# The last block of a cross-attention kernel, taken in two halves of its queries

## The chip, the cores and the metric

One Trainium2 chip, one of its cores. The metric is the device time of one execution in microseconds (us). TensorE (PE) multiplies matrices, VectorE (DVE), ScalarE (ACT) and GpSimd (POOL) work on the elements of a tile, and the queues of SyncE (SP) and ScalarE issue the transfers (DMA). Each engine runs its own list of instructions in the order in which they are written, and semaphores tie the lists together: an instruction whose semaphore isn't there yet holds everything behind it on its engine.

## What is computed

Cross-attention of 4 x 1024 queries on 77 keys for each batch, 16 heads of 16 columns, all in float32:

```
q, k, v = x W_Q^T, ctx W_K^T, ctx W_V^T          x: (4, 1024, 256), ctx: (4, 77, 256), 16 heads of 16
scores  = q k^T / 4,  -1e9 where mask == 1
p       = softmax(scores)
concat  = p v                                     (4, 1024, 256)
out     = concat W_O^T + x
result  = (out - mean) * rsqrt(var + 1e-5) * gamma + beta      (mean and var over the 256 columns)
```

## The kernel before

The 4096 queries are cut into 8 **blocks** of 512 (n = 0 to 7, N = 8). A block has 16 heads, worked off in 8 **steps** of two heads (a pair), and in 4 **quads** of four heads (t = 0 to 3). Engines work on several blocks at once. For the last two blocks only this matters:

- **Scores** (PE, L912, `scores`): two matmuls a step, keys on the partitions, 512 queries as columns, into two of six PSUM banks. The last steps rotate over three pairs of banks (`pair_bank`), so step k waits for the exponentials of step k - 3 (`heads_gone`).
- **Exponentials** (ACT, L551, `exp`): one instruction for the 77 x 1024 scores of a pair, to `probs`.
- **Values** (PE, L920, `values`): four matmuls, one for each head of a quad, into the four strips of 32 partitions of the one bank `pv_ps`. The sum of the exponentials comes along as an extra column of v. The next quad may write `pv_ps` only when DVE has transposed the one before out of it.
- **Turn** (DVE, L670 and L672, `turn`): `pv_ps` is transposed in squares of 32 to `ctx_q`, and the reciprocals of the sums are taken. **Norm** (POOL, L364, `norm`) multiplies the two into `ctx_n`. **Turn back** (DVE, L678, `turn_back`) transposes two quads (one of two column halves) to `ctx_e`.
- **Output** (PE, L930, `project_out`): 4 fp32 matmuls for each half of the rows, into the bank `work_ps`. **Residual** (DVE, L684) adds x from `y`. **Stats** (DVE, L690 and L695) take mean and variance.
- **Moments** (POOL, L373 to L378): four small instructions make 1/sqrt(var + eps) and the shift. **Apply** (ACT, L557) scales and shifts the four tiles of a block. **Times gamma** (POOL, L385) and **plus beta** (POOL, L391), two instructions each for a block. SP then stores the block (`store_y`, L282).

The last block (n = 7) ends in another way. Its fourth quad is taken in two halves of 256 queries, in two PSUM banks (`last_values`, L1048), and DVE does the whole way of each half itself: transpose, reciprocal, product, transpose back (`turn_last`, L707 to L715). The output matmuls (L1053) go into four PSUM tiles `last_ps`, x is added by a matmul with the identity (L1057), and DVE does statistics, gamma and beta on PSUM (L811 to L827). POOL gives only 1/sqrt(var + eps) for each half (L485). The block is stored in two halves from ACT's queue (L614).

The order of the work around the end is written out by hand, for each engine. POOL, from the last norm of block 6 on: moments(5), norm(7, 0), plus beta(4), times gamma(5) first half, norm(7, 1), times gamma(5) second half, norm(7, 2), moments(6), times gamma(6) in both halves, the two L485, plus beta(6) in both halves. Plus beta(5) is on DVE (L700), ahead of the last quad. SP stores blocks 5 and 6 when their plus beta is done.

Of the kernel before, what the change touches and what calls it, by code (L numbers as in the profile page):

```python
# [8 lines left out]
ALU = mybir.AluOpType  # L9
# [3 lines left out]
P = 128  # L13
BATCH = 4
SEQ = 1024
D = 256
# [44 lines left out]
Y_RING = 4  # L61
R_RING = 3
# [52 lines left out]
def cross_attention(nc, x, x_cols, ctx_cols, mask_cols, w_q, w_k, w_v, w_o, gamma, beta, out):  # L115
    stack = ExitStack()
    with stack:
# [6 lines left out]
        def sem(name):  # L124
            return stack.enter_context(nc.semaphore(name))
# [61 lines left out]
        last_ps = [banks[:, 0, 0:D], banks[:, 1, 0:D], work_ps[:, 0:D], banks[:, 2, 0:D]]  # L187

        last_pv = [pv_ps[:, 0:BLOCK // 2], banks[:, 3, 0:BLOCK // 2]]
# [25 lines left out]
        ident_ready, last_scaled, last_shifted = sem("ident_ready"), sem("last_scaled"), sem("last_shifted")  # L215
        last_bn, last_mv, last_ve, last_rstd = sem("last_bn"), sem("last_mv"), sem("last_ve"), sem("last_rstd")
# [120 lines left out]
        def _(pool):  # L337
# [132 lines left out]
            norm(N - 2, 3)  # L470
            moments(N - 3)
            norm(N - 1, 0)
            plus_beta(N - 4, 1)
            times_gamma(N - 3, 0)
            norm(N - 1, 1)
            times_gamma(N - 3, 1)
            norm(N - 1, 2)

            moments(N - 2)
            for half in range(2):  # L480
                times_gamma(N - 2, half)
            for half in range(2):
                two = slice(2 * half, 2 * half + 2)
                pool.wait_ge(last_ve, half + 1)
                nc.gpsimd.tensor_tensor(rstd_last[:, two], var_eps_last[:, two], minus_half[:, two], ALU.pow).then_inc(last_rstd, 1)  # L485
            for half in range(2):
                plus_beta(N - 2, half)
# [4 lines left out]
        def _(act):  # L492
# [92 lines left out]
            for n in range(N):  # L585
                for s in range(STEPS):
# [19 lines left out]
                    at = {N - 2: 5, N - 1: 3}.get(n, 6)  # L606
                    if s in (at, at + 1) and n >= 2:
                        for t in (2 * (s - at), 2 * (s - at) + 1):
                            apply(n - 2, t)
            for t in range(TILES):  # L610
                apply(N - 2, t)
# [8 lines left out]
        def _(dve):  # L620
# [76 lines left out]
            def plus_beta(m, half):  # L697
                rows = y[m % Y_RING][:, 2 * half:2 * half + 2, :]
                dve.wait_ge(y_gamma, 2 * m + half + 1)
                nc.vector.tensor_tensor(rows, rows, beta_sb[:, :].unsqueeze(1).to_broadcast([P, 2, D]), ALU.add).then_inc(y_beta, 1)  # L700

            def turn_last(half):
                chunks = slice(half * CHUNKS // 2, (half + 1) * CHUNKS // 2)
                m, t = N - 1, QUADS - 1
                dve.wait_ge(pv_done, QUADS * m + t + half + 1)
                dve.wait_ge(ctx_normed, QUADS * m + t)
                nc.vector.transpose(ctx_q[:, t % 2, chunks, :], last_pv[half]).then_inc(pv_turned, 1)  # L707
                dve.wait_ge(pv_turned, QUADS * m + t + half + 1)
                nc.vector.reciprocal(rden[:, t % 2, chunks], ctx_q[:, t % 2, chunks, DK]).then_inc(rden_ready, 1)
                dve.wait_ge(rden_ready, QUADS * m + t + half + 1)  # L710
                nc.vector.tensor_tensor(ctx_n[:, 1, chunks, DK:2 * DK], ctx_q[:, t % 2, chunks, 0:DK],
                                        rden[:, t % 2, chunks].unsqueeze(2).to_broadcast([P, CHUNKS // 2, DK]),
                                        ALU.mult).then_inc(ctx_normed, 1)
                dve.wait_ge(ctx_normed, QUADS * m + t + half + 1)
                nc.vector.transpose(ctx_e[m % 2][:, 1, half * BLOCK // 2:(half + 1) * BLOCK // 2], ctx_n[:, 1, chunks, :]  # L715
                                    ).then_inc(ctx_e_ready, 1)
# [77 lines left out]
            turn(n, 0)  # L794
            residual(n - 1, 0)
            turn(n, 1)
            stats(n - 1, 0)
            turn_back(n, 0)
            residual(n - 1, 1)
            turn(n, 2)  # L800
            stats(n - 1, 1)
            for half in range(2):
                plus_beta(n - 2, half)
            for half in range(2):
                turn_last(half)
            m, rows = n, y[n % Y_RING]
            for half in range(2):
                two = slice(2 * half, 2 * half + 2)
                for t in (2 * half, 2 * half + 1):
                    dve.wait_ge(out_done, 2 * m + t + 1)  # L810
                    nc.vector.bn_stats(bn_last[:, t, :], last_ps[t]).then_inc(last_bn, 1)  # L811
                    dve.wait_ge(last_bn, t + 1)
                    nc.vector.bn_aggr(mean_var_last[:, t, :], bn_last[:, t, :]).then_inc(last_mv, 1)
                dve.wait_ge(last_mv, 2 * half + 2)
                nc.vector.tensor_scalar(var_eps_last[:, two], mean_var_last[:, two, 1], EPS, None, ALU.add).then_inc(last_ve, 1)
                if half == 0:
                    for t in range(2):
                        nc.vector.scalar_tensor_tensor(out=last_ps[t], in0=last_ps[t], scalar=mean_var_last[:, t, 0:1],
                                                       in1=gamma_sb[:, :], op0=ALU.subtract, op1=ALU.mult).then_inc(last_scaled, 1)
            for t in (2, 3):  # L820
                nc.vector.scalar_tensor_tensor(out=last_ps[t], in0=last_ps[t], scalar=mean_var_last[:, t, 0:1],
                                               in1=gamma_sb[:, :], op0=ALU.subtract, op1=ALU.mult).then_inc(last_scaled, 1)
            for half in range(2):
                dve.wait_ge(last_rstd, half + 1)
                for t in (2 * half, 2 * half + 1):
                    dve.wait_ge(last_scaled, t + 1)
                    done = nc.vector.scalar_tensor_tensor(out=rows[:, t, :], in0=last_ps[t], scalar=rstd_last[:, t:t + 1],  # L827
                                                          in1=beta_sb[:, :], op0=ALU.mult, op1=ALU.add)
                done.then_inc(last_shifted, 1)
# [4 lines left out]
        def _(pe):  # L834
# [210 lines left out]
            def last_values(half):  # L1045
                cols = slice(half * BLOCK // 2, (half + 1) * BLOCK // 2)
                for j in range(4):
                    last = nc.tensor.matmul(last_pv[half][32 * j:32 * (j + 1), :], v_all[:, n // PER_BATCH, 4 * (QUADS - 1) + j, :],  # L1048
                                            probs[:, 2 * (QUADS - 1) + j // 2, j % 2, cols], start=True, stop=True)
                last.then_inc(pv_done, 1)  # L1050

            def last_out(v, t):
                return nc.tensor.matmul(last_ps[t], ctx_e[n % 2][:, v, t * P:(t + 1) * P], wo_t[:, v, :],  # L1053
                                        start=(v == 0), stop=(v == HALVES - 1))

            def last_residual(t):
                nc.tensor.matmul(last_ps[t], ident32[:, :], rows[:, t, :], start=False, stop=False)  # L1057

            scores(n, 0)
            scores(n, 1)  # L1060
            values(n - 1, 3)
            scores(n, 2)
            values(n, 0)
            scores(n, 3)
            pe.wait_ge(out_ready, 2 * (n - 1))
            project_out(n - 1, 0)
            scores(n, 4)
            values(n, 1)
            scores(n, 5)
            pe.wait_ge(out_ready, 2 * (n - 1) + 1)  # L1070
            project_out(n - 1, 1)
            scores(n, 6)
            values(n, 2)
            scores(n, 7)
            pe.wait_ge(s_x[n % Y_RING], 16 * (n // Y_RING + 1))
            pe.wait_ge(ident_ready, 1)
            pe.wait_ge(exp_done, HEADS * n + 12)
            pe.wait_ge(ctx_e_ready, HALVES * n + 1)
            last_out(0, 0)
            last_out(0, 1)  # L1080
            pe.wait_ge(exp_done, HEADS * N)
            pe.wait_ge(pv_turned, QUADS * n + QUADS - 1)
            last_values(0)
            last_values(1)
            last_residual(0)
            last_residual(1)
            for t in range(TILES):
                if t == 2:
                    pe.wait_ge(out_ready, 2 * n)
                if t >= 2:  # L1090
                    last_out(0, t)
                    last_residual(t)
                if t % 2 == 0:
                    pe.wait_ge(ctx_e_ready, HALVES * n + 2 + t // 2)
                last_out(1, t).then_inc(out_done, 1)
# [39 lines left out]
```

## Time and profile before

| | |
|---|---|
| median of 3 runs | 186.15 us (182.85, 186.15, 188.56) |
| the profiled execution, its own time | 182.77 us |
| its span, first to last instruction | 181.0 us |
| granted TensorE clock, mean over the span | 0.976 of 2.4 GHz |
| PE busy | 159.6 us (88%), 1224 matmuls |
| DVE busy | 136.9 us (76%), 305 instructions |
| ACT busy | 103.2 us (57%), 188 instructions |
| POOL busy | 102.5 us (57%), 125 instructions |

The shares are means over the whole span, and most of the span is the same loop over blocks. The change touches the last 30 us. There the timelines of the engines and the chain of waits are read: a timeline line gives the start, the duration of the merged piece, the operation with its tiles, the number of instructions, and in brackets how long the engine had sat idle before it and what released it. Busy times of neighbours on one engine overlap a little, since an instruction starts before the one in front of it has ended; the distance between two starts is what an instruction costs in a row of others.

### The profile page before, as it was taken

The page shows a single profiled execution, that of the slowest core. Times are in us where ns is not written, and L with a number is a line of the kernel's source. Part 1 is how long each engine was busy: PE and PEld are TensorE (multiplying, and loading weights), DVE is VectorE, ACT ScalarE, POOL GpSimd, SP SyncE. Part 2 cuts the span into 40 slices and gives each one's busy share as a digit, 9 for nine tenths or more (in the row PEclk, how much of TensorE's full clock was granted, in tenths as well). Part 3 has the DMA queues.
Part 4 walks back from the last instruction along what each step waited for, and adds up shares of the span by engine and source line. Part 5 has one row for each costly group of instructions (what it writes and reads, how often), then busy time and mean ns, then how long its engine had stood idle before and what let it go on. Part 6 is the DMA issues. An engine that isn't in the chain of part 4 may idle for free.

```text
span 181.0 us, 3572 instructions
## 1 busy us (share of the span) xinstructions
PE 159.6 (88%) x1224; PEld 87.9 (49%) x1224; DVE 136.9 (76%) x305; ACT 103.2 (57%) x188; POOL 102.5 (57%) x125
## 2 busy tenths in 40 slices
PE   7698877889579999999999999999999897999830
PEld 7455534444244565456545654565366462264520
DVE  0779755885958579788978897889989966748990
ACT  3224154673366565658765876587777659586400
POOL 7000761242835451448597959754954787865692
PEclk9999999999999999999999999999999999699995
DMA  4949947779867987973686665647551033020205
GB/s 158 384 120 184 257 86 224 182 167 230 188 170 217 281 237 216 253 201 85 196 274 181 193 198 145 187 164 205 141 182 53 4 121 116 0 116 4 116 0 232
DMA packets 21829, 30.17 MB, mean 167 GB/s; under 512 B 3436, under 2 KB 17356, under 8 KB 21812
## 3 DMA queue, kind: packets, MB, share of 16 engines
q1 hardware_dynamic: 20692, 28.19, 55.8%
q10 hardware_dynamic: 1120, 1.76, 2.9%
q8 instruction: 10, 0.16, 0.4%
q14 instruction: 7, 0.06, 0.1%
HBM read 11.28 MB, written 4.19 MB: 85 GB/s over the span
## 4 chain that ended last, share of the span: by engine, by line
PE 52%; DVE 12%; POOL 9%; issue 9%; DMA 8%; ACT 6%; ACTq 1%; POOLq 0%; SPq 0%; DVEq 0%
PE pv_ps L920 12%; PE work_ps L857 11%; PE work_ps L930 9%; PE scores_ps L912 9%; PE scores_ps L878 6%; DMA R<-neg_max_t 4%; DMA x_t<-in_x_cols 4%; POOL y L385 3%; DVE ctx_q L670 2%; PE scores_ps L857 2%; DVE neg_max L662 2%; DVE q L651 2%; POOL rstd L376 2%; POOL ctx_n L364 2%; DVE bn L690 1%
## 5 line engine op out<-in xcount | busy, mean ns | idle before, releaser
L547 ACT ACTIVATE probs<-scores_ps 77x512 f32<-77x512 f32 x108 | 57.7, 589 | 36.7 <-PE scores_ps L912 31.4
L662 DVE TENSOR_REDUCE neg_max<-scores_ps 128x6 f16<-128x462 f32 (+1 forms) x84 | 45.2, 565 | 11.0 <-PE scores_ps L878 11.0
L912 PE MATMUL scores_ps<-R,kb 126*77 126x512 f16 x128 | 39.5, 388 | 4.1 <-DMA R<-neg_max_t 3.0
L357 POOL TENSOR_TENSOR q<-q 128x512 f16<-128x512 f32 x14 | 16.2, 1161 | 43.4 <-ACT q L505 43.4
L878 PEld LDWEIGHTS scores_ps<-kb,R 125*128 125x128 f16 x512 | 26.7, 98 | 28.5 <-DVE neg_max L662 10.8
L920 PE MATMUL pv_ps<-probs,v_all 77*32 77x512 f32 x248 | 33.8, 618 | 2.2 <-ACT probs L551 1.0
L364 POOL TENSOR_TENSOR ctx_n<-ctx_q,rden 128x256 f32<-128x256 f32 x31 | 19.5, 628 | 23.6 <-DVE rden L672 23.5
L878 PE MATMUL scores_ps<-kb,R 125*128 125x77 f16 x512 | 31.2, 199 | 1.3 <-DVE neg_max L662 1.1
L670 DVE STREAM_TRANSPOSE ctx_q<-pv_ps 128x512 f32<-128x512 f32 x31 | 22.1, 712 | 9.3 <-PE pv_ps L920 8.9
L930 PE MATMUL work_ps<-wo_t,ctx_e 128*128 128x256 f32 x112 | 27.4, 388 | 0.0
L857 PE MATMUL work_ps<-x_t,wq_t 128*128 128x512 f32 x48 | 23.6, 614 | 0.4
L930 PEld LDWEIGHTS work_ps<-wo_t,ctx_e 128*128 128x128 f32 x112 | 21.3, 194 | 3.5 <-issue 0.2
L385 POOL TENSOR_TENSOR y<-y,gamma_sb 128x512 f32<-128x512 f32 x14 | 17.8, 1274 | 2.8 <-ACT y L557 2.8
L912 PEld LDWEIGHTS scores_ps<-R,kb 126*77 126x77 f16 x128 | 11.2, 117 | 15.8 <-issue 5.8
L557 ACT ACTIVATE y<-y,shift,rstd 128x256 f32<-128x256 f32 x28 | 15.1, 591 | 2.9 <-POOL shift L378 2.9
L391 POOL TENSOR_TENSOR y<-y,beta_sb 128x512 f32<-128x512 f32 x12 | 15.2, 1269 | 0.0
L505 ACT ACTIVATE q<-q 128x512 f16<-128x512 f32 x16 | 10.0, 626 | 7.5 <-DVE q L651 5.5
L551 ACT ACTIVATE probs<-scores_ps 77x1024 f32<-77x1024 f32 x10 | 9.9, 1016 | 4.1 <-PE scores_ps L912 4.1
L684 DVE TENSOR_TENSOR y<-work_ps,y 128x512 f32<-128x512 f32 x14 | 9.5, 680 | 3.6 <-PE work_ps L930 3.6
L342 POOL TENSOR_SCALAR eq<-mask_i 77x512 f16<-77x512 int32 x6 | 11.6, 1929 | 1.0 <-DMA mask_i<-in_mask_cols 1.0
L857 PEld LDWEIGHTS work_ps<-x_t,wq_t 128*128 128x128 f32 x48 | 8.2, 190 | 6.6 <-issue 5.7
L678 DVE STREAM_TRANSPOSE ctx_e<-ctx_n 128x512 f32<-128x512 f32 x15 | 10.5, 703 | 1.0 <-POOL ctx_n L364 1.0
(88 smaller groups left out, 158.7 us busy)
## 6 DMA issues: line engine op xcount, KB each, us to landing
R<-mask_t SPq DMA_DIRECT2D x12, 616.0 KB
R<-q SPq DMA_DIRECT2D x48, 128.0 KB
x_t<-in_x_cols SPq DMA_DIRECT2D x8, 512.0 KB, 6.2
y<-in_x SPq DMA_DIRECT2D x8, 512.0 KB, 4.6
out<-y SPq DMA_DIRECT2D x7, 512.0 KB, 2.6
mask_i<-in_mask_cols SPq DMA_DIRECT2D x8, 154.0 KB
out<-y ACTq DMA_DIRECT2D x2, 256.0 KB, 2.0
kb<-k SPq DMA_DIRECT2D x12, 38.5 KB, 2.9
```

The lines of the kernel that those rows point to most:

```text
L357: nc.gpsimd.tensor_tensor(q16[:, e, 1, :], q32[:, e, :], q16[:, e, 0, :], ALU.subtract).then_inc(q_low, 1)
L364: nc.gpsimd.tensor_tensor(ctx_n[:, v, :, u * DK:(u + 1) * DK], ctx_q[:, t % 2, :, 0:DK], rden[:, t % 2, :].unsqueeze(2).to_broadcast([P, C ...
L385: nc.gpsimd.tensor_tensor(rows, rows, gamma_sb[:, :].unsqueeze(1).to_broadcast([P, 2, D]), ALU.mult).then_inc(y_gamma, 1)
L391: nc.gpsimd.tensor_tensor(rows, rows, beta_sb[:, :].unsqueeze(1).to_broadcast([P, 2, D]), ALU.add).then_inc(y_beta, 1)
L547: nc.scalar.activation(probs[:, s, head % 2, :], banks[0:KEYS, head % SCORES_RING, :], ACT.Exp).then_inc(exp_done, 1)
L662: nc.vector.tensor_reduce(to[:, t, lo:hi], max_ps[u % MAX_RING][:, 0:(hi - lo) * KEYS].rearrange("p (h k) -> p h k", k=KEYS), AX.X, ALU.ma ...
L670: nc.vector.transpose(ctx_q[:, t % 2, :, :], pv_ps[:, :]).then_inc(pv_turned, 1)
L857: last = nc.tensor.matmul(bank, wq_t[:, t, e * P:(e + 1) * P], x_t[m % X_RING][:, t, :], start=(t == 0), stop=(t == HALVES - 1))
L878: last = nc.tensor.matmul(max_ps[u % MAX_RING][:, (h - lo) * KEYS:(h - lo + 1) * KEYS], R[m % R_RING][0:MAX_ROW, h, t * P:(t + 1) * P], kb ...
L912: nc.tensor.matmul(banks[0:KEYS, bank, :], kb[:, 2 * s + i, n // PER_BATCH, :], R[n % R_RING][:, 2 * s + i, :], start=True, stop=True).the ...
L920: last = nc.tensor.matmul(pv_ps[32 * j:32 * (j + 1), :], v_all[:, n // PER_BATCH, 4 * t + j, :], probs[:, 2 * t + j // 2, j % 2, :], start ...
L930: last = nc.tensor.matmul(work_ps[:, i * D:(i + 1) * D], ctx_e[n % 2][:, v, q0:q0 + P], wo_t[:, v, :], start=(v == 0), stop=(v == HALVES - 1))
```

## The change

Block 7 goes through its four quads twice: parts g = 0 to 3 are the quads for the first 256 queries, g = 4 to 7 the same quads for the other 256.

- PE: each `part_scores` has four matmuls of 256 columns (a part's four heads fill the same two banks that a pair filled before), each `part_values` four of 256 columns, into the first half of `pv_ps`. A part's values wait for the transposition of the part before. Once parts 0 to 3 are turned back (`part_e` 1 and 2), x and the output matmuls of the first half go to `work_ps`; those of the second half to a pair of score banks.
- ACT: eight exponentials of 77 x 1024, as before, each writing half of the queries of four heads. The applies of block 5 follow parts 3 and 4.
- DVE: eight half-size turns and four half-size turn-backs; the product of the last part alone is DVE's. `last_moments(0)` stands ahead of turn 7, `last_shift(0)` behind the last turn-back.
- POOL: seven half-size norms, plus beta(5) moved here from DVE, and another order: the two times gamma of block 6 come after the first L485, and the second L485 between the two plus beta of block 6.

The core of the diff:

```
 (POOL)
-            norm(N - 1, 0)
+            norm_part(0)
             plus_beta(N - 4, 1)
-            norm(N - 1, 1) ... norm(N - 1, 2)
-            moments(N - 2)
-            for half in range(2):
-                times_gamma(N - 2, half)
-            for half in range(2):
-                ... rstd_last ...
-            for half in range(2):
-                plus_beta(N - 2, half)
+            norm_part(1)
+            times_gamma(N - 3, 0)
+            norm_part(2)
+            norm_part(3)
+            times_gamma(N - 3, 1)
+            norm_part(4)
+            moments(N - 2)
+            norm_part(5)
+            plus_beta(N - 3, 0)
+            norm_part(6)
+            plus_beta(N - 3, 1)
+            rstd_of_last(0)
+            for half in range(2):
+                times_gamma(N - 2, half)
+            plus_beta(N - 2, 0)
+            rstd_of_last(1)
+            plus_beta(N - 2, 1)

 (DVE)
-            turn(n, 0); residual(n - 1, 0); turn(n, 1); stats(n - 1, 0); turn_back(n, 0)
-            residual(n - 1, 1); turn(n, 2); stats(n - 1, 1); plus_beta(n - 2, 0 and 1)
-            turn_last(0); turn_last(1); ... statistics and outputs of the last block
+            turn_part(0)
             residual(n - 1, 0)
+            turn_part(1)
+            turn_back_part(0, 0)
+            turn_part(2)
+            residual(n - 1, 1)
+            turn_part(3)
             stats(n - 1, 0)
+            turn_back_part(0, 1)
+            turn_part(4)
             stats(n - 1, 1)
+            turn_part(5)
+            turn_back_part(1, 0)
+            turn_part(6)
+            last_moments(0)
+            turn_part(7)
+            norm_last_part()
+            turn_back_part(1, 1)
+            last_shift(0)
+            last_moments(1)
+            last_shift(1)

 (PE)
+            part_scores(0); part_scores(1); values(n - 1, 3); part_scores(2); part_values(0); part_scores(3)
+            project_out(n - 1, 0); part_values(1); part_scores(4); project_out(n - 1, 1)
+            part_values(2); part_scores(5); part_values(3); part_scores(6); part_values(4); part_scores(7)
+            last_x(0, work_ps)                      # x of both tiles of the first half
+            last_out(0, 0); last_out(0, 1)
+            part_values(5)
+            last_out(1, 0); last_out(1, 1)          # after part_e 2
+            part_values(6)
+            last_x(2, ...); last_x(3, ...)
+            last_out(0, 2); last_out(0, 3)          # after part_e 3
+            part_values(7)
+            last_out(1, 2); last_out(1, 3)          # after part_e 4
```

## Rows read from the trace of the kernel before

**Rows 1.** Chain that ended last, order of time: start us, us, what; final links.
```profile
171.12 2.50 POOL y L385 x2
173.62 0.66 POOL rstd_last L485
...
175.32 2.45 POOL y L391 x2
```

**Rows 2.** Timeline of the queues: block 6's store, block 7's two; page, to landing.
```profile
177.80 0.33 SPq L282 DMA_DIRECT2D out<-y  x1
...
176.14 1.13 ACTq L614 DMA_DIRECT2D out<-y  x2
...
out<-y ACTq DMA_DIRECT2D x2, 256.0 KB, 2.0
```

**Rows 3.** Timeline of POOL, 156 to 175 us.
```profile
156.27 0.23 POOL L373 TENSOR_SCALAR var_eps<-mean_var 128x4 f32<-128x4 f32 x1 [0.21 <-DVE mean_var L695]
...
158.21 0.62 POOL L364 TENSOR_TENSOR ctx_n<-ctx_q,rden 128x256 f32<-128x256 f32 x1
...
167.34 0.58 POOL L373 TENSOR_SCALAR var_eps<-mean_var 128x4 f32<-128x4 f32 x1 [0.21 <-DVE mean_var L695]
...
168.60 1.04 POOL L376 TENSOR_TENSOR rstd<-var_eps,minus_half 128x4 f32<-128x4 f32 x1
169.71 0.20 POOL L378 TENSOR_TENSOR shift<-rstd,neg_mean 128x4 f32<-128x4 f32 x1
...
174.63 0.70 POOL L485 TENSOR_TENSOR rstd_last<-var_eps_last,minus_half 128x2 f32<-128x2 f32 x1 [0.35 <-DVE var_eps_last L815]
```

**Rows 4.** Timeline of PE, 153 to 170 us.
```profile
153.22 1.06 PE L920 MATMUL pv_ps<-probs,v_all 77*32 77x512 f32 x8 [1.04 <-ACT probs L551]
...
155.22 1.86 PE L920 MATMUL pv_ps<-probs,v_all 77*32 77x512 f32 x8 [0.38 <-DVE ctx_q L670]
...
157.88 2.34 PE L930 MATMUL work_ps<-wo_t,ctx_e 128*128 128x256 f32 x8
...
162.03 1.89 PE L930 MATMUL work_ps<-wo_t,ctx_e 128*128 128x256 f32 x8
163.76 0.60 PE L912 MATMUL scores_ps<-R,kb 126*77 126x512 f16 x2
...
167.10 0.64 PE L1048 MATMUL pv_ps<-probs,v_all 77*32 77x256 f32 x8 [0.33 <-ACT probs L551]
167.56 0.61 PE L1048 MATMUL scores_ps<-probs,v_all 77*32 77x256 f32 x8
```

**Rows 5.** Windows: stretch, length, busy of each engine, granted clock, DMA share, GB/s.
```profile
154.00:160.00 6.00, 5.62 (x24) 2.64 (x21) 3.39 (x9) 3.78 (x6) 5.12 (x8) 0.72 0.00 0
```

**Rows 6.** Timeline of DVE, 162 to 170 us.
```profile
162.63 0.69 DVE L690 BATCH_NORM_STATS2 bn<-y 128x6 f32<-128x256 f32 x2
...
163.46 0.71 DVE L678 STREAM_TRANSPOSE ctx_e<-ctx_n 128x512 f32<-128x512 f32 x1
164.09 0.65 DVE L684 TENSOR_TENSOR y<-work_ps,y 128x512 f32<-128x512 f32 x1
...
167.17 1.26 DVE L700 TENSOR_TENSOR y<-y,beta_sb 128x512 f32<-128x512 f32 x2
168.35 0.44 DVE L707 STREAM_TRANSPOSE ctx_q<-pv_ps 128x256 f32<-128x256 f32 x1
168.82 0.20 DVE L709 RECIPROCAL rden<-ctx_q 128x8 f32<-128x8 f32 x1
169.06 0.29 DVE L711 TENSOR_TENSOR ctx_n<-ctx_q,rden 128x128 f32<-128x128 f32 x1
169.38 0.45 DVE L715 STREAM_TRANSPOSE ctx_e<-ctx_n 128x256 f32<-128x256 f32 x1
```

**Rows 7.** Timeline of DVE, 27 to 47 us: two runs of L719, the same size.
```profile
27.77 0.47 DVE L719 TENSOR_SCALAR kb<-ident 77x1232 f16<-77x1232 f16 x1
...
46.55 0.86 DVE L719 TENSOR_SCALAR kb<-ident 77x1232 f16<-77x1232 f16 x1
```

More of the change, by code:

```diff
@@ L583, in _ @@
             turn_first_max(1)
-            for n in range(N):
+            for n in range(N - 1):
                 for s in range(STEPS):
@@ new lines, in turn_part @@
+            def turn_part(g):
+                half, t = g // QUADS, g % QUADS
+                chunks = slice(half * HALF_CHUNKS, (half + 1) * HALF_CHUNKS)
+                dve.wait_ge(part_pv, g + 1)
+                if g < 2:
+                    dve.wait_ge(ctx_normed, QUADS * (N - 2) + t + 3)
+                elif t >= 2:
+                    dve.wait_ge(part_normed, g - 1)
+                nc.vector.transpose(ctx_q[:, t % 2, chunks, :], pv_ps[:, 0:HALF]).then_inc(part_turned, 1)
+                dve.wait_ge(part_turned, g + 1)
+                nc.vector.reciprocal(rden[:, t % 2, chunks], ctx_q[:, t % 2, chunks, DK]).then_inc(part_rden, 1)
@@ new lines, in last_moments @@
+            def last_moments(half):
+                two = slice(2 * half, 2 * half + 2)
+                for t in (2 * half, 2 * half + 1):
+                    dve.wait_ge(last_out_done, 2 if half == 0 else t + 1)
+                    nc.vector.bn_stats(bn_last[:, t, :], last_ps[t]).then_inc(last_bn, 1)
+                for t in (2 * half, 2 * half + 1):
+                    dve.wait_ge(last_bn, t + 1)
+                    nc.vector.bn_aggr(mean_var_last[:, t, :], bn_last[:, t, :]).then_inc(last_mv, 1)
+                dve.wait_ge(last_mv, 2 * half + 2)
+                nc.vector.tensor_scalar(var_eps_last[:, two], mean_var_last[:, two, 1], EPS, None, ALU.add).then_inc(last_ve, 1)
+                for t in (2 * half, 2 * half + 1):
+                    nc.vector.scalar_tensor_tensor(out=last_ps[t], in0=last_ps[t], scalar=mean_var_last[:, t, 0:1],
+                                                   in1=gamma_sb[:, :], op0=ALU.subtract, op1=ALU.mult).then_inc(last_scaled, 1)
@@ new lines, in last_shift @@
+            def last_shift(half):
+                dve.wait_ge(last_rstd, half + 1)
+                for t in (2 * half, 2 * half + 1):
+                    dve.wait_ge(last_scaled, t + 1)
+                    done = nc.vector.scalar_tensor_tensor(out=y[(N - 1) % Y_RING][:, t, :], in0=last_ps[t],
+                                                          scalar=rstd_last[:, t:t + 1], in1=beta_sb[:, :],
+                                                          op0=ALU.mult, op1=ALU.add)
+                done.then_inc(last_shifted, 1)
@@ L804, in _ @@
[L804 to L829, printed above, removed]
+            turn_part(5)
@@ L1056, in last_residual, with part_scores @@
[L1056 to L1060, printed above, removed]
+            def part_scores(g):
+                half, t = g // QUADS, g % QUADS
+                if g == 0:
+                    pe.wait_ge(s_nm, 16 * n)
+                if g < 3:
+                    pe.wait_ge(exp_done, heads_gone(PAIRS * n + g))
+                else:
+                    pe.wait_ge(part_exp, g - 2)
+                for j in range(4):
+                    done = nc.tensor.matmul(part_ps[g][0:KEYS, j // 2, (j % 2) * HALF:(j % 2 + 1) * HALF],
+                                            kb[:, 4 * t + j, n // PER_BATCH, :],
+                                            R[n % R_RING][:, 4 * t + j, half * HALF:(half + 1) * HALF], start=True, stop=True)
+                done.then_inc(part_scored, 1)
@@ new lines, in part_values @@
+            def part_values(g):
+                half, t = g // QUADS, g % QUADS
+                if g == 0:
+                    pe.wait_ge(pv_turned, QUADS * n)
+                else:
+                    pe.wait_ge(part_turned, g)
+                pe.wait_ge(part_exp, g + 1)
+                for j in range(4):
+                    done = nc.tensor.matmul(pv_ps[32 * j:32 * (j + 1), 0:HALF], v_all[:, n // PER_BATCH, 4 * t + j, :],
+                                            probs[:, 2 * t + j // 2, j % 2, half * HALF:(half + 1) * HALF], start=True, stop=True)
+                done.then_inc(part_pv, 1)
@@ L1061, in _, with last_x, last_out @@
+            def last_x(lo, to):
+                tiles = rows[:, lo:lo + to.shape[-1] // D, :]
+                nc.tensor.matmul(to, ident32[:, :], tiles, start=True, stop=False)
+            def last_out(v, t, stop=False):
+                return nc.tensor.matmul(last_ps[t], ctx_e[n % 2][:, v, t * P:(t + 1) * P], wo_t[:, v, :], start=False, stop=stop)
+            part_scores(0)
+            part_scores(1)
             values(n - 1, 3)
-            scores(n, 2)
-            values(n, 0)
-            scores(n, 3)
+            part_scores(2)
@@ L1098 @@
+            pe.wait_ge(part_e, 2)
+            last_out(1, 0)
+            last_out(1, 1, stop=True).then_inc(last_out_done, 2)
+            part_values(6)
+            last_x(2, last_ps[2])
+            last_x(3, last_ps[3])
+            pe.wait_ge(part_e, 3)
+            last_out(0, 2)
+            last_out(0, 3)
+            part_values(7)
+            pe.wait_ge(part_e, 4)
+            for t in (2, 3):
+                last_out(1, t, stop=True).then_inc(last_out_done, 1)
 def kernel(**inputs):
```

128 lines of the change are left out of this document (63 added, 65 removed).

## The prediction

> **What bounds the kernel now.** I read the tail alone, since nothing ahead of block 7's first values changes. The chain of waits shows the end: applies of block 6 on ACT, then on POOL times gamma, an inverse root, plus beta [rows 1]. Plus beta ends at 177.77 us, SP issues the store at 177.80 [rows 2], and the span ends at 181.0: 3.23 us from the last POOL instruction to the end. Block 7's own second store is issued by 177.27 [rows 2] and lands 2.0 us later [rows 2]: 179.3, 1.7 us of slack. So **the end belongs to block 6 and to POOL**, not to block 7, which the change is about. The timelines of POOL, PE and DVE give the durations; the windows give the clock, whose mean from 154 to 160 us is 0.72 [rows 5]. With the levels 1.2 and 2.4 GHz that is 3.4 us at the lower one; values that take 1.86 us instead of 1.06 at 155.22 and a projection of 2.34 instead of 1.89 at 157.88 [rows 4] put it at about 155.3 to 158.7, after PE had idled 1.04 and 0.38 us [rows 4]. PE's work up to 155.2 stays the same, so I keep this stretch where it is.
>
> **PE up to the second projection.** Before, the first half of block 6's projection starts at 157.88 and the second at 162.03 [rows 4]: 4.15 us for it, two score steps and one quad of values. In front of it now stands a half-size part. At full clock a quad is 1.06 us and a half 0.64, with 0.46 between the starts of two halves [rows 4]; at half clock that is 0.9 instead of 1.8. So the projection starts 1.0 us earlier, at 156.9 (its input, block 6's second turn-back, is there at 156.8 as before), but loses 0.5 of that by running longer at half clock. Between the two projections one quad has become a part (-0.5) and one score step has gone behind (-0.5). The second projection then starts at 157.9 - 1.0 + 0.5 + 4.15 - 1.0 = 160.5 and ends 1.73 later (start distance, [rows 4]), at 162.2: **1.5 us earlier than before**. Eight exponentials of the same size and the same columns of scores are no change; ACT waits on PE here and hides its own work.
>
> **DVE to the statistics of block 6.** Behind the projection come values 2 (0.64, ends 162.9) and on DVE, back to back: turn 2, residual, turn 3, stats half 0, turn-back, turn 4, stats half 1. A half turn costs 0.47 to its reciprocal and about 0.13 for that, 0.6 [rows 6]; residual 0.6, stats 0.83, half turn-back 0.37 to 0.45 (all [rows 6]); the last stats take 1.0 to their end. Sum: 3 x 0.6 + 0.6 + 0.83 + 0.37 + 1.0 = 4.6, so the statistics end at 167.5. Before, moments of block 6 start at 167.34 [rows 3]; now at **167.6, +0.25**. The lead of 1.5 us is eaten by two more half turns and a turn-back ahead of the statistics.
>
> **POOL from there to the end** is the sum that decides. Against before:
>
> - moments of block 6: 2.57 us before (167.34 to 169.91), but 1.94 for the same four instructions of block 5 (156.27 to 158.21) [rows 3]. The slow ones lay beside DVE's plus beta (167.17 to 168.43, [rows 6]), which is gone: -0.6.
> - norm parts 5 and 6 now stand behind moments. A norm of 256 elements takes 0.62 [rows 3], one of 512 elements (gamma, beta) 1.25 [rows 1], so time goes with elements: 0.31 to 0.35 each, bounds 0.31 and 0.62. I take 0.35, as POOL's 4-element instruction still takes 0.20: +0.7.
> - plus beta of block 5, moved here from DVE, where it took 1.26: two of 1.24 [rows 1]: **+2.5**.
> - gamma waited for the applies, which wait for moments: moments end 169.91, gamma starts 171.12 [rows 3, 1]. Now the norms and plus beta fill that gap: -1.2.
> - the second root waited 0.35 for DVE [rows 3]; now it stands behind the first plus beta of block 6: -0.35.
>
> From 167.6: 1.95 + 0.35 + 1.23 + 0.35 + 1.23 + 0.66 (root) + 2.46 (gamma) + 1.23 + 0.66 + 1.25 = 11.4, so POOL ends at 179.0, against 177.77: 0.25 - 0.6 + 0.7 + 2.5 - 1.2 - 0.35 = +1.3, +1.2 by start times. Stores as before, 3.23 us. But the two stores (block 7's second half at 178.7, block 6 at 179.0) now lie 0.3 apart, where it was 0.9; between nothing and 0.3 for that, I take 0.1: **+1.3 us**. Store of block 5 is issued at 172.8, clear of both.
>
> **Block 7's own path**, to see that it stays inside. First half: part 5's norm waits on POOL until moments are done (169.5), the turn-back behind it starts at 169.9, turn 6 behind that at 170.3. Statistics and scaling of the first half follow (its outputs stood ready from 168.8), then turn 7 at 172.8, DVE's product and turn-back (0.20 + 0.29 + 0.45 and latencies, [rows 6]) to 174.3. PE, idle for 2.5 us, does the last outputs (two of a projection's four tile products, half of its 1.73 us, and 0.16 to the end) by 175.4. Variance of the second half at 176.3, but POOL takes its root only at 177.05, behind plus beta: 0.8 us of slack. The shifts end at 178.7, the store is issued by 179.05 and lands at 181.05, 1.1 us ahead of the other.
>
> **The sum**: profiled execution 182.77 + 1.3 = 184.1 us. That execution is near the fastest of the three runs (182.85); their median is 186.15, 3.4 us higher for reasons that no trace shows, so I carry the difference over: **187.4 us**, +0.7%. A measurement of this kernel tells about 2% (3.7 us) from no change.
>
> **Rivals.**
>
> 1. *The last round trip becomes the bound.* DVE's product (ctx_q times rden, two SBUF inputs) at 173.5 falls in POOL's times gamma (173.4 to 174.6). For a block between the two: one L719 took 0.86 us instead of 0.47 [rows 7], and POOL's small L373 0.58 instead of 0.23 while DVE ran plus beta [rows 3, 6]. Against: L711 ran in its 0.29 us inside POOL's 1.04 us root [rows 3, 6]. If it waits out the gamma, +1.1 us; and if PE's clock falls in the then 3.6 us of idleness, these two products cost 0.86 more. It decides once both exceed the 0.8 us of slack: +1.2 on the forecast, 188.6 us. The Trainium skill ("SBUF — State Buffer", section "SBUF: two separate sides") says that such a DVE instruction and a GpSimd one that reads SBUF exclude each other for a whole instruction; by it the wait occurs and the sum is the 188.6 of this rival if the clock falls too, 187.8 if not. The trace agrees in L719 and L373, and speaks against in L711.
> 2. *Slower by over 2%: half pieces cost what whole ones do.* Eight trips PE to DVE to PE go over one bank. At whole-size prices the four parts of values ahead of the statistics cost 0.5 more each, the four turns 0.3, norm parts 5 and 6 0.27: 2.0 + 1.2 + 0.5 = 3.7, less some 0.3 where PE waits anyway: 3.4 over my forecast, 190.8. With whole-size turns and norms it passes 2% once the values of a part start 0.7 us apart. Against: halves took 0.61 to 0.64 [rows 4] and 0.44 [rows 6] where wholes take 1.06 and 0.71.
> 3. *The waits on POOL close up.* POOL's work from the first norm part (158.2, [rows 3]) is 7 x 0.35 + 9 x 1.24 + 1.95 + 2 x 0.68 = 16.9 us; my schedule has 3.8 us of waits in 20.8. Without any, the end is 158.2 + 16.9 + 3.2 = 178.3, 2.6 us under before: 183.5 us. For it: the statistics could come earlier if the lower clock does not fall there. Against: the norm parts wait on PE, in order. Even this floor is only 1.4%: **a gain over 2% has no place** in this tail.
>
> **Chances.** Forecast within half a microsecond or so 0.50; rival 1 0.21; rival 3, in part or whole, 0.15; rival 2 0.12; something else 0.02. Range 183.5 (rival 3) to 190.0: rival 1 at 188.6 with norms at their upper bound (+0.5) and values parts 0.6 apart (+0.4) on top, 189.5, and 0.5 for a stretch of lower clock; rival 2 is left out. Faster by over 2%: 0.08, only from the scatter of the runs. Slower by over 2%: rival 2 and the rest of the scatter, 0.14. Within 2%: 0.78.
>
> **What would show it.** In the new profile: POOL without a gap over 0.2 us from its moments of block 6 (167 to 168) to its last plus beta (near 179), and the chain ending in that plus beta and SP's store; the moments in 1.95 us; norm parts near 0.35; the second projection starting near 160.5; L719-like stretching of DVE's last product, or not; PE idle for 2 to 3 us before its last two tiles. I am wrong if block 7's store ends the span, if POOL still waits before its gamma, or if the statistics of block 6 end before 166.5 or after 168.5.

## The result and the profile after

The changed kernel took 189.45 us (median of 4 executions, 188.75 to 189.72), the kernel before 185.09 us (median of 4, 182.85 to 188.56): ratio 1.0281, 95% interval 1.0233 to 1.0330. **Slower by 2.8%**, where +0.7% was forecast. Medians, here and below, take every execution; the ratios and their intervals leave out those more than 1.5% above the fastest of their kernel. The profiled execution took 189.72 us with a span of 187.6 us, against 182.77 and 181.0.

To compare the tails, both are counted from one event that the change leaves alone: the start of PE's values for the last quad of block 6, at 153.22 us before [rows 4]. In the changed kernel (timeline of PE):

```profile
157.42 1.07 PE L976 MATMUL pv_ps<-probs,v_all 77*32 77x512 f32 x8 [1.03 <-ACT probs L578]
...
164.07 1.89 PE L986 MATMUL work_ps<-wo_t,ctx_e 128*128 128x256 f32 x8
...
175.30 0.64 PE L1123 MATMUL pv_ps<-probs,v_all 77*32 77x256 f32 x8
179.08 2.04 PE L1132 MATMUL scores_ps<-wo_t,ctx_e 128*128 128x256 f32 x4 [3.15 <-DVE ctx_e L763]
```

That start is 4.2 us late. Two score steps of the changed block 7 have run by then (155.35), but these values wait for an exponential of block 6, and the delay is much older: the same values of an early block start at 56.36 us before and at 60.55 in the changed kernel, where nothing has been changed yet. The **tail**, from there to the end of the span, is 30.2 us, where it was 27.8. So 6.6 us between two profiles fall into 4.2 ahead of the change and 2.4 behind it. The 4.2 are the clock; windows of the changed kernel (stretch, length, busy time of PE, PEld, DVE, ACT and POOL, granted clock, DMA share, GB/s):

```profile
40.00:50.00 10.00, 7.17 (x52) 3.18 (x52) 7.11 (x14) 3.61 (x7) 5.54 (x5) 0.97 0.79 215
50.00:60.00 10.00, 9.21 (x42) 3.89 (x43) 3.40 (x6) 3.36 (x6) 2.88 (x3) 0.52 0.74 210
```

The clock fell from its level of 2.4 GHz to that of 1.2 GHz at about 49.5 us, while PE waited 3.35 us for the row of maxima of block 1, and came back at about 59.6; in the profile of before it stayed up there, after a wait of 3.00 us, and fell at 155 us [rows 5].

In the tail, POOL's timeline is the one to hold against [rows 3] and [rows 1]:

```profile
171.17 0.23 POOL L381 TENSOR_SCALAR var_eps<-mean_var 128x4 f32<-128x4 f32 x1 [0.45 <-DVE mean_var L732]
...
173.06 0.40 POOL L485 TENSOR_TENSOR ctx_n<-ctx_q,rden 128x128 f32<-128x128 f32 x1
173.42 1.28 POOL L399 TENSOR_TENSOR y<-y,beta_sb 128x512 f32<-128x512 f32 x1
...
175.01 1.28 POOL L399 TENSOR_TENSOR y<-y,beta_sb 128x512 f32<-128x512 f32 x1
176.39 0.71 POOL L492 TENSOR_TENSOR rstd_last<-var_eps_last,minus_half 128x2 f32<-128x2 f32 x1
177.07 2.53 POOL L393 TENSOR_TENSOR y<-y,gamma_sb 128x512 f32<-128x512 f32 x2
179.56 1.26 POOL L399 TENSOR_TENSOR y<-y,beta_sb 128x512 f32<-128x512 f32 x1
182.09 0.71 POOL L492 TENSOR_TENSOR rstd_last<-var_eps_last,minus_half 128x2 f32<-128x2 f32 x1 [1.27 <-DVE var_eps_last L775]
182.77 1.26 POOL L399 TENSOR_TENSOR y<-y,beta_sb 128x512 f32<-128x512 f32 x1
```

POOL works without a break of note from 171.17 to 180.82, as forecast, and then waits 1.27 us for the variance of block 7's second half, with half of block 6's plus beta queued behind the root. DVE shows why that variance is late:

```profile
175.39 0.92 DVE L775 TENSOR_SCALAR var_eps_last<-mean_var_last 128x2 f32<-128x2 f32 x1
...
177.72 0.76 DVE L750 TENSOR_TENSOR ctx_n<-ctx_q,rden 128x128 f32<-128x128 f32 x1
178.58 0.45 DVE L763 STREAM_TRANSPOSE ctx_e<-ctx_n 128x256 f32<-128x256 f32 x1
...
181.84 0.17 DVE L775 TENSOR_SCALAR var_eps_last<-mean_var_last 128x2 f32<-128x2 f32 x1
```

The same instruction on two elements takes 0.92 us beside POOL's plus beta (175.01 to 176.29) and 0.17 when POOL does nothing; the last product takes 0.76 us beside times gamma, where it took 0.29 [rows 6]. PE idles 3.15 us and does its last two fp32 matmuls (a row counts each as two, x4) in 2.04 us; the same in the middle of the tail took 1.03 (170.22 us). Block 6's store is the last: POOL ends at 184.03, the span at 187.6.

### The profile page after: what moved, and what is told of

Same layout as the page of the kernel before. It is cut to its first block, busy times and chain, and to the rows that moved or that the text cites. A ratio compares the mean times of both kernels' runs of the same rounds, so it can differ in the third digit from the quotient of the medians.

```text
span 187.6 us, 3661 instructions
## 1 busy us (share of the span) xinstructions
PE 164.4 (88%) x1262; PEld 90.4 (48%) x1262; DVE 137.5 (73%) x309; ACT 103.4 (55%) x188; POOL 105.0 (56%) x131
## 4 chain that ended last, share of the span: by engine, by line
PE 51%; DVE 13%; POOL 11%; DMA 9%; issue 9%; ACT 3%; SPq 1%; POOLq 0%; ACTq 0%; DVEq 0%
PE work_ps L913 12%; PE pv_ps L976 10%; PE work_ps L986 9%; PE scores_ps L968 8%; PE scores_ps L934 6%; DMA R<-neg_max_t 4%; DMA x_t<-in_x_cols 3%; POOL y L393 3%; POOL ctx_n L372 2%; DMA R<-q 2%; PE scores_ps L913 2%; POOL y L399 2%; DVE neg_max L699 2%; DVE ctx_q L707 2%; POOL rstd L384 2%
## 5 line engine op out<-in xcount | busy, mean ns | idle before, releaser
L934 PEld LDWEIGHTS scores_ps<-kb,R 125*128 125x128 f16 x512 | 27.5, 100 | 30.0 <-DVE neg_max L699 10.8
L968 PE MATMUL scores_ps<-R,kb 126*77 126x512 f16 x112 | 35.4, 393 | 4.5 <-DMA R<-neg_max_t 3.4
L934 PE MATMUL scores_ps<-kb,R 125*128 125x77 f16 x512 | 31.9, 201 | 1.4 <-DVE neg_max L699 1.1
L976 PE MATMUL pv_ps<-probs,v_all 77*32 77x512 f32 x224 | 30.7, 621 | 1.8 <-ACT probs L578 1.0
L372 POOL TENSOR_TENSOR ctx_n<-ctx_q,rden 128x256 f32<-128x256 f32 x28 | 17.6, 627 | 21.4 <-DVE rden L709 21.4
L707 DVE STREAM_TRANSPOSE ctx_q<-pv_ps 128x512 f32<-128x512 f32 x28 | 19.9, 710 | 8.4 <-PE pv_ps L976 8.0
L913 PE MATMUL work_ps<-x_t,wq_t 128*128 128x512 f32 x48 | 25.3, 653 | 0.4
L399 POOL TENSOR_TENSOR y<-y,beta_sb 128x512 f32<-128x512 f32 x14 | 17.8, 1271 | 0.0
L968 PEld LDWEIGHTS scores_ps<-R,kb 126*77 126x77 f16 x112 | 9.8, 119 | 11.3 <-ACT probs L574 3.9
L727 DVE BATCH_NORM_STATS2 bn<-y 128x6 f32<-128x256 f32 x28 | 10.0, 398 | 0.0
```

The source lines that it names most:

```text
L372: nc.gpsimd.tensor_tensor(ctx_n[:, v, :, u * DK:(u + 1) * DK], ctx_q[:, t % 2, :, 0:DK], rden[:, t % 2, :].unsqueeze(2).to_broadcast([P, C ...
L707: nc.vector.transpose(ctx_q[:, t % 2, :, :], pv_ps[:, :]).then_inc(pv_turned, 1)
L913: last = nc.tensor.matmul(bank, wq_t[:, t, e * P:(e + 1) * P], x_t[m % X_RING][:, t, :], start=(t == 0), stop=(t == HALVES - 1))
L934: last = nc.tensor.matmul(max_ps[u % MAX_RING][:, (h - lo) * KEYS:(h - lo + 1) * KEYS], R[m % R_RING][0:MAX_ROW, h, t * P:(t + 1) * P], kb ...
L968: nc.tensor.matmul(banks[0:KEYS, bank, :], kb[:, 2 * s + i, n // PER_BATCH, :], R[n % R_RING][:, 2 * s + i, :], start=True, stop=True).the ...
L976: last = nc.tensor.matmul(pv_ps[32 * j:32 * (j + 1), :], v_all[:, n // PER_BATCH, 4 * t + j, :], probs[:, 2 * t + j // 2, j % 2, :], start ...
```

## Experiments

Times are medians; the column beside them has the median of the kernel before, run in the same set, and kernels of different sets are best compared by their distance from it. The tail is taken from each profile.

| kernel | median us | before, same set | block 6's last values start | span | tail |
|---|---|---|---|---|---|
| before, first profile | 185.09 | (itself) | 153.22 | 181.0 | 27.8 |
| before, again | 184.47 | 184.52 | 156.34 | 182.8 | 26.5 |
| b_warm | 182.11 | 184.36 | 154.38 | 180.8 | 26.4 |
| b_warm2 | 183.29 | 184.52 | 155.40 | 181.8 | 26.4 |
| b_poolbeta | 182.67 | 184.83 | 152.74 | 179.7 | 27.0 |
| changed, first profile | 189.45 | 185.09 | 157.42 | 187.6 | 30.2 |
| changed, again | 188.56 | 184.83 | 156.67 | 186.9 | 30.2 |
| a_warm | 185.64 | 184.36 | 153.20 | 183.0 | 29.8 |
| a_beta | 185.26 | 184.36 | 154.15 | 183.9 | 29.75 |
| a_root | 184.62 | 184.36 | 153.00 | 181.9 | 28.9 |
| a_pve | 185.58 | 184.83 | 154.10 | 183.5 | 29.4 |
| a_tailwarm | 186.01 | 184.83 | 156.61 | 185.9 | 29.3 |
| a_best | 184.85 | 184.52 | 153.92 | 183.2 | 29.3 |
| a_full | 184.35 | 185.13 | 153.58 | 182.4 | 28.8 |

**The early wait, b_warm and a_warm.** The same edit in both kernels:

```
 scores(n, s), elif s == 0:
+    if n == 1:
+        pe.wait_ge(exp_done, HEADS + 1 - SCORES_RING)
+        for _ in range(40):
+            nc.tensor.matmul(banks[:, HEADS % SCORES_RING, 0:P], zeros16[:, :], zeros16[:, :], start=True, stop=True)
     pe.wait_ge(s_nm, 16 * n)
```

> The kernel before, with 40 small matmuls of zeros put on PE in its first long wait (47.5 to 50.7 us, for the row of negative maxima of block 1), into a score bank that is free; nothing that is computed changes. Theory A (PE's clock falls in this wait in some executions, whatever the last block does, and that made 4.2 of the 6.6 us between the two profiles): the clock stays up at 47 to 60 us, the time is that of the fastest executions, 182.5 to 183.5 us, with little scatter. Theory B (the wait has nothing to do with the difference, the change itself slows the whole program): no change in the median, 185 us, scatter as before.

> The changed kernel with the same 40 small matmuls in the same wait. Theory A: block 6's last values start near 153.2 us again (157.4 in the changed kernel without them) and the time falls by 4.2 us, to about 185.4 us; what is left over the kernel before with the same matmuls is the tail alone, 2.4 us by the two profiles (1.3 us was forecast for it). Theory B: still 189 us.

182.11 us (ratio to before 0.9877, 0.9804 to 0.995) and 185.64 us (1.0083, 1.004 to 1.0127). The changed kernel's values start at 153.20 again: the 4.2 us are the clock's (mean 1.00 from 50 to 60 us, where it was 0.52), theory A holds. Between the two: 3.5 us of medians, 3.4 of tail, more than the 2.4 of the first pair of profiles. b_warm has the lowest median of all, 2.25 us under the kernel before of its set.

**Both kernels again.**

> The changed kernel as it is, once more beside the kernel before, for the granted clock of every execution. Theory A1 (the early fall of the clock at 49 us is a matter of the single execution): part of the executions near 185.3 us with a mean clock of 0.97 or more, as with the matmuls of zeros in the early wait, the others near 189.5 with 0.955; the median of many comes down to 186 to 188. Theory A2 (the changed program meets the fall in every execution): all near 189.4 us with 0.955.

> The kernel before, unchanged, as a kernel of its own: a second profile of it. Theory A1 (the early wait for the row of negative maxima is as long in both kernels and the clock falls by chance): a wait of 2.6 to 3.8 us, as in all profiles taken so far. Theory A3 (the early wait is longer in the changed kernel: 3.35 and 3.48 us, against 3.00, and just past what the clock stands): again 2.9 to 3.1 us, with the clock up, and mean clocks of 0.973 to 0.985 in most executions.

The changed kernel: 188.56 us, single executions 185.67, 187.29, 188.10, 189.01, 189.61 and 191.98, so it is probably not bound to the fall; but the lowest had a mean clock of 0.968, not the 0.97 of A1, the median lies above A1's 186 to 188, and only the first, at 189.01, has a profile (ratio 1.0135, 1.0061 to 1.0208). The kernel before: 184.47 us, and A3 as it was put, with the clock up, is refuted. Timeline of PE, kernel before, second profile:

```profile
50.84 1.07 PE L912 MATMUL scores_ps<-R,kb 126*77 126x512 f16 x2 [3.12 <-DMA R<-neg_max_t]
...
52.23 1.94 PE L920 MATMUL pv_ps<-probs,v_all 77*32 77x512 f32 x8
...
156.34 1.06 PE L920 MATMUL pv_ps<-probs,v_all 77*32 77x512 f32 x8 [1.04 <-ACT probs L551]
```

Here **the kernel before meets the early fall too**, after 3.12 us of waiting (still less than the 3.35 and 3.48 of the changed kernel), and its values start at 156.3. The later fall is missing, and the tail is 26.5 us, as in b_warm and b_warm2. So the first profile of before, on which the forecast stood, had its fall in the tail (27.8 us); this one, at 184.58 us, lies at the median.

**One part alone in the old kernel, b_poolbeta.**

```
 (DVE)  -            for half in range(2): plus_beta(n - 2, half)
 (POOL)              moments(N - 2)
        +            plus_beta(N - 3, 0); plus_beta(N - 3, 1)
```

> b_warm (the kernel before with matmuls of zeros in the early wait) with one part of the change alone: plus beta of block 5 moved from DVE to POOL, behind moments of block 6. The forecast's terms: +2.5 for the two additions, -1.2 for the wait for the applies that they fill, -0.6 for the moments that no longer lie beside DVE's additions: +0.7 us over b_warm, up to 1.3 if the moments stay slow. If POOL's work were not the bound of the old tail: 0.

182.67 us, +0.56 on b_warm, but only 0.1 by the distances from the kernel before of each set (-2.16, -2.25); the tail decides, 26.96 against 26.42, +0.54. Timelines of POOL and DVE:

```profile
165.56 0.23 POOL L373 TENSOR_SCALAR var_eps<-mean_var 128x4 f32<-128x4 f32 x1 [0.21 <-DVE mean_var L697]
...
167.44 2.55 POOL L391 TENSOR_TENSOR y<-y,beta_sb 128x512 f32<-128x512 f32 x2
169.95 2.48 POOL L385 TENSOR_TENSOR y<-y,gamma_sb 128x512 f32<-128x512 f32 x2
...
170.44 0.80 DVE L815 TENSOR_SCALAR var_eps_last<-mean_var_last 128x2 f32<-128x2 f32 x1
```

Moments fast, the wait filled, 2.5 us added: three terms of the forecast's sum stand. The run also shows the collisions in the old last block, where only this part of the change is in: DVE's L815 took 0.17 us before (172.31) and takes 0.80 beside times gamma. Of DVE's two last products, 0.29 us each before, the second (168.12) takes 0.74 beside plus beta, the first (166.75) still 0.29 beside POOL's small root.

**The other way, a_beta**: plus beta of block 5 back on DVE in a_warm.

> The one before this, with plus beta of block 5 back on DVE (one half ahead of turn 5, one behind it) and off POOL. Theory C (the tail is late because of a chain that goes through DVE's variance and last product, which wait for POOL's long instructions, and through PE's restart at the lower clock): only 0.5 to 1.0 us better than a_warm, since the last product is freed by some 0.9 us and nothing else. Theory D (POOL's amount of work is the bound, as forecast): 2.0 to 2.5 us better.

Tail 29.75 us, nothing gained on 29.8; the median 0.4 lower. POOL spends what it was relieved of in waits:

```profile
171.67 0.40 POOL L485 TENSOR_TENSOR ctx_n<-ctx_q,rden 128x128 f32<-128x128 f32 x1 [1.13 <-DVE rden L747]
172.72 0.70 POOL L492 TENSOR_TENSOR rstd_last<-var_eps_last,minus_half 128x2 f32<-128x2 f32 x1 [0.65 <-DVE var_eps_last L778]
...
178.45 0.71 POOL L492 TENSOR_TENSOR rstd_last<-var_eps_last,minus_half 128x2 f32<-128x2 f32 x1 [1.30 <-DVE var_eps_last L778]
```

POOL's amount of work alone, the bound of my forecast, is refuted as the bound of the changed tail. Theory C's half microsecond came and was lost again: PE's last matmuls start 0.4 us earlier than in a_warm (21.25 against 21.66 after block 6's last values), but take 2.07 us, where the clock in a_warm fell only half way through them (1.64).

**The root behind both plus beta, a_root.**

```
             plus_beta(N - 2, 0)
-            rstd_of_last(1)
             plus_beta(N - 2, 1)
+            rstd_of_last(1)
```

> a_warm with POOL's root for the second half of block 7 put behind both plus beta of block 6, not between them. Theory C: the root came late anyway (POOL waited 1.27 us for the variance), so it loses nothing, block 6's store leaves 1.9 us earlier and block 7's second store ends the span: 1.3 to 1.6 us better than a_warm. Theory D (POOL's work back to back is the bound, the root's place is worth only its own 0.7 us for block 6 and costs block 7 0.5 us): 0.3 us better or less.

184.62 us, 1.0 under a_warm, tail 28.9, 0.9 under it: less than the 1.3 of theory C, three times theory D. Block 6 no longer waits for block 7's variance. Timelines of PE, DVE and POOL:

```profile
174.66 1.13 PE L1136 MATMUL scores_ps<-wo_t,ctx_e 128*128 128x256 f32 x4 [3.14 <-DVE ctx_e L763]
...
176.51 1.14 DVE L775 TENSOR_SCALAR var_eps_last<-mean_var_last 128x2 f32<-128x2 f32 x1
...
177.73 0.71 POOL L492 TENSOR_TENSOR rstd_last<-var_eps_last,minus_half 128x2 f32<-128x2 f32 x1
```

What theory C left out is that block 7's root now stands behind all of plus beta, which ends at 177.62 us; the shift behind it, and the store that ends the span, follow. L775 collides again (1.14 us) but ends at 177.65, with that plus beta, so by itself it cost less than 0.1 us.

**PE kept busy in its last wait, a_tailwarm**: 45 matmuls of zeros behind `part_values(7)` in a_warm.

> a_warm with 45 more small matmuls of zeros on PE in its last long wait (before the last two output products), into a score bank that is free. Theory C (the restart at the lower clock is one link of the chain that sets the end): the last four fp32 matmuls take 1.0 to 1.1 us, not 1.6 to 2.0, POOL's wait for the variance (0.86 to 1.3 us) nearly vanishes, 0.6 to 0.9 us better than a_warm. Theory D (POOL's amount of work is the bound): no difference.

```profile
175.06 2.69 PE L1175 MATMUL scores_ps<-zeros 128*128 128x128 f16 x45
178.28 1.13 PE L1136 MATMUL scores_ps<-wo_t,ctx_e 128*128 128x256 f32 x4 [0.53 <-DVE ctx_e L763]
```

1.13 us instead of 2.04, POOL's wait 0.35; tail 29.3, 0.9 under the changed kernel, but 0.5 under a_warm, in whose restart the clock fell half way (1.64 us). The medians hardly show it (186.01, which is 1.18 over the kernel before, where a_warm is 1.28 over): single executions lie between 183.97 and 188.00.

**var + eps on POOL, a_pve** (in a_warm).

```
 rstd_of_last: +  nc.gpsimd.tensor_scalar(var_eps_last[:, two], mean_var_last[:, two, 1], EPS, None, ALU.add)
 last_moments: -  nc.vector.tensor_scalar(var_eps_last[:, two], mean_var_last[:, two, 1], EPS, None, ALU.add)
```

> a_warm with var + eps of block 7 taken from DVE (L775) and given to POOL, in front of its root. Theory E (DVE's small instruction and its last product each waited for a long POOL instruction on SBUF to end): DVE has no 0.9 us instruction any more, turn 7 starts 0.75 us earlier, the last product falls before POOL's times gamma and takes 0.3 us, not 0.76, PE waits some 2 us, not 3.1, and its clock stays up; 0.5 to 1.0 us better than a_warm though POOL has 0.6 us more to do. Rival F (the two are slow for a reason of their own, no collision): the last product still takes 0.76 us, and the time is 0 to 0.6 us worse.

```profile
173.57 0.29 DVE L752 TENSOR_TENSOR ctx_n<-ctx_q,rden 128x128 f32<-128x128 f32 x1
...
174.47 2.07 PE L1137 MATMUL scores_ps<-wo_t,ctx_e 128*128 128x256 f32 x4 [1.85 <-DVE ctx_e L765]
```

The product, now beside POOL's root and no longer beside gamma (which starts at 174.04), takes 0.29 us; PE waits 1.85 us. That is theory E, but the clock fell all the same, and the tail gains 0.4; the median is 0.75 over the kernel before, where a_warm is 1.28 over.

**All of it, a_best and a_full.** a_best: matmuls of zeros in three waits, var + eps on POOL, root last. a_full: plus beta on DVE as well. b_warm2: b_warm with 18 matmuls of zeros ahead of block 6's last values.

> b_warm with 18 more small matmuls of zeros on PE in the wait of 1.0 us ahead of block 6's last values, after which the clock fell in the profile of the kernel before (154 to 160 us, mean 0.72). If that fall costs 1.4 us where it happens: the median falls to 181.5 us or less and the executions lie closer together, about 2.8 us under the kernel before. If the fall at 155 us is rare in b_warm anyway: 182.1 us as b_warm.

> The changed kernel with all that helped it: matmuls of zeros in the three long waits of PE (40, 18 and 25), var + eps of block 7 on POOL, its second root behind both plus beta of block 6. Theory C (with POOL's wait and DVE's collisions gone the end is set by POOL's work and then by block 7's shift and store, some 29 us after block 6's last values start): 183.5 us, 1.5 to 2 us under a_warm and still 1.5 to 2 us over b_warm2. Rival G (the two halves pay once the collisions are gone): as fast as b_warm2 or faster.

> a_best with plus beta of block 5 back on DVE as well, so that POOL has 2.5 us less to do in the tail. Measured as the time from the start of block 6's last values to the end of the span, which is 26.4 us in the kernel before and 30.2 in the changed one with the clock up, 29.3 in a_best. Theory C (two bounds stand behind each other: POOL's work, and the last part's values, which PE issues 4.7 us after their exponentials since turn 6 stands behind a turn-back that waits for POOL): 28.4 to 28.8 us, with block 7's own store at the end. Theory D (POOL's amount of work alone): 27 us or less.

b_warm2: 183.29 us, 180.53 to 184.78, not the 181.5 expected; its tail is b_warm's. The profile lost its time to other falls, between 25 and 35 us; with 4 and 6 executions the two are not told apart. a_best 184.85 us, tail 29.3: the miss is that the root, last now, holds block 7's shift for 2.8 us. a_full 184.35 us (ratio 0.9941, 0.9908 to 0.9973), tail 28.8, theory C. **No arrangement brought the changed tail under 28.8 us, 2.4 over the old one.** Timelines of PE and DVE in a_full:

```profile
171.57 0.64 PE L1133 MATMUL pv_ps<-probs,v_all 77*32 77x256 f32 x8
...
173.41 0.97 DVE L755 TENSOR_TENSOR ctx_n<-ctx_q,rden 128x128 f32<-128x128 f32 x1
...
174.98 1.13 PE L1142 MATMUL scores_ps<-wo_t,ctx_e 128*128 128x256 f32 x4 [1.27 <-DVE ctx_e L768]
...
178.97 0.88 DVE L788 SCALAR_TENSOR_TENSOR y<-scores_ps,rstd_last,beta_sb 128x256 f32<-128x256 f32 x2 [1.25 <-POOL rstd_last L494]
```

The product collides again (0.97 us), since turn 7 comes later than POOL's root. But it doesn't set the end here: DVE waits 1.25 us for the second root, which stands behind POOL's gamma and plus beta (172.97 to 177.95 us), and these stand behind the first root, for which POOL had waited 0.45 us.

## Why the prediction was wrong

The mechanism named first was right: block 6's store ends the span, POOL's added work goes in front of it, block 7's gain is worth nothing. The size was 1.3 us; it is 3.7 us of tail with the clock up in both (30.2 against 26.5). Its terms, second profile of before against the first of after:

| term | forecast | measured | from (before, after) |
|---|---|---|---|
| moments of block 6 start, after block 6's last values | +0.25 | +0.94 | 12.81, 13.75 |
| moments themselves | -0.6 | -0.63 | 2.58, 1.94 |
| norm parts 5 and 6 | +0.7 | +0.7 | 0.36 each from start to start |
| plus beta of block 5 | +2.5 | +2.5 | b_poolbeta: 2.5 |
| wait for the applies | -1.2 | -1.2 | 1.20, none |
| second root's wait | -0.35 | +0.92 | 0.35, 1.27 |
| the end's store | +0.1 | +0.36 | 3.21, 3.57 |

The measured terms add up to 3.6 of the 3.7 us.

- **The step that failed is the term for the second root's wait: it waited 0.35 for DVE and was to wait no more behind the first plus beta of block 6, -0.35, with 0.8 us of slack.** The wait did not vanish, it grew to 1.27. That was rival 1, with a chance of 0.21. It had both its links: the product waited 0.47 us for gamma, and PE's restart cost 1.0 us. With 4.2 us taken off for the late start, the second half's variance is ready at 177.8, not 176.3, and POOL is through with its first plus beta at 176.6, not 177.05. a_tailwarm and a_pve show the links one by one; neither alone sets the end. The rival's price of +1.2 came out (-0.35 to +0.92), but by luck: the product lost 0.47 and not 1.1, the restart 1.0 and not 0.86, and POOL was 0.4 earlier. What I had not seen was a third link, L775, 0.75 us at 175.39, ahead of turn 7; turn 7 came at the time forecast all the same (172.8), since the statistics of block 6 were 0.6 us earlier than forecast.
- The Trainium skill ("SBUF — State Buffer", section "SBUF: two separate sides") says that a DVE instruction that reads SBUF twice and a GpSimd one that reads SBUF exclude each other for a whole instruction. The trace agrees in the product: 0.76 to 0.97 us beside gamma, 0.29 beside the root of two elements (a_pve), and 0.74 beside plus beta (b_poolbeta). I had counted L711 beside such a root as evidence against; it is none, for it shows only that this small instruction does not block. L719, which I had counted for it, reads one tensor and not two.
- **The base was one execution with its clock fall in the tail.** I kept that fall in both kernels, where it put PE's second projection and block 6's moments 1.3 us later in the old kernel (8.81 against 7.51 and 14.12 against 12.81). In the changed profile it does not occur there (mean 1.00 from 154 to 160 us), nor in the second profile of before. The measured -0.37 for the start of moments in the first pair (14.12, 13.75) hides +0.94. With the clock up PE's second projection is 0.86 us earlier (7.51, 6.65), not 1.5. From there to the moments the forecast had 7.1 us and 7.10 were measured (5.30 before). So DVE's longer list was right, and the lead it eats was too large.
- The store: 0.3 us between the two last stores cost 0.36, a little over its upper bound of 0.3.
- Rival 2 is out: values parts took 0.64 us, half turns 0.41 to 0.45, norm parts 0.36 to 0.41. Rival 3 is out: POOL's waits moved, they did not close up.

Why the change has nothing to give: the exponentials of part 7 end at 170.58 us in the changed kernel and its values start at 175.30, 4.7 us later, where before the values of the last quad followed at once (idle 0.33, [rows 4]). PE does not wait in between, it works off its own list (timeline of PE):

```profile
170.22 1.03 PE L1132 MATMUL work_ps<-wo_t,ctx_e 128*128 128x256 f32 x4
171.17 0.64 PE L1123 MATMUL pv_ps<-probs,v_all 77*32 77x256 f32 x8
171.74 1.13 PE L1132 MATMUL work_ps<-wo_t,ctx_e 128*128 128x256 f32 x4
172.80 0.64 PE L1123 MATMUL pv_ps<-probs,v_all 77*32 77x256 f32 x8
173.37 1.13 PE L1129 MATMUL scores_ps<-y,ident 128*128 128x256 f32 x4
174.34 1.03 PE L1132 MATMUL scores_ps<-wo_t,ctx_e 128*128 128x256 f32 x4
```

The outputs of the first half and x of the second, which stood behind the last values before, now stand in front of them. DVE's turn 6 is no bound here, though the turn-back ahead of it waits 0.93 us for POOL's norm part 5: it is over at 174.28. So the reason that the expectation of a_full gives for these 4.7 us is wrong. Behind the values turn 7 then waits on DVE until 177.01, for the first half's variance (with L775) and scaling. The first half's statistics do run beside the second half, but they, its outputs and the turn-backs are now in front of the last quad. That chain is read from the traces; no run took it apart, and PE's list was tried in no other order.

Open: the medians of the first set differ by 4.4 us and of the second by 3.7, the tails by 3.7. Whether the changed kernel meets the early fall more often than the old one is not settled; b_again shows only that both do. Not tried: times gamma of block 6 ahead of norm part 6 and the first root, in whose place POOL waits 1.13 and 0.45 us in a_full.

## What to carry to other kernels

Find the block whose store ends last before you speed up another one. A wait that moves behind something long is only gone if what it waits for does not move too: price the chain of the producer (its collisions, the restart of an idle PE) and not the consumer's queue alone. Before a forecast rests on one profile, see whether a clock fall lies in the stretch, and count from an event ahead of the change: two profiles of one kernel differed by 1.8 us in span and 3.1 us in where the tail began, while three tails of the old last block with the clock up (before again, b_warm, b_warm2) agreed to 0.1 us.

## What the runs showed of the hardware

- In the early wait of four profiles PE's clock stayed up over 3.00 us and fell in waits of 3.12, 3.35 and 3.48 us. At the end of the tail it had fallen by the time PE went on after 1.85 us (a_pve, 2.07 us for the last matmuls) and 2.63 us (a_beta, 2.07), fell half way through them after 3.14 us (a_warm, 1.64), and was up all through them after 3.14 us in a_root (1.13). So the length of one wait does not tell it.
- A DVE `tensor_scalar` on 128 x 2 elements took 0.17 us alone, and 0.92 and 1.14 us beside a POOL addition of about 1.26 us (the changed kernel, a_root). It ended within 0.05 us of that addition's end both times.
- 40 matmuls of zeros in the 3 us wait took 2.40 us of idle PE time and 2.25 us off the median of the kernel before (b_warm).
